# A fused attention and FFN kernel on eight cores: two FFN steps instead of one after an attention unit, and the attention epilogue due after 12 units instead of 14

## What is computed

```python
def reference(L0_attn_x, L0_attn_Wc_down, L0_attn_Wq_up, L0_attn_Wkv_up, L0_attn_Wc_proj,
              L0_ffn_w_gate, L0_ffn_w_up, L0_ffn_w_down):
    # x: (2, 8192, 1024) float32
    # attention: latent = x @ Wc_down (1024 -> 512); q = latent @ Wq_up (16 heads of 64);
    # one k and one v of 64 for all heads = latent @ Wkv_up; causal softmax(q k / 8) v;
    # then @ Wc_proj
    # ffn: h = silu(x @ wg.T) * (x @ wu.T), 3072 wide, then h @ wd.T; int weights times 1/127
    x = L0_attn_x
    xn = _layernorm(x, axis=-1)
    s = _L0_attn_ref(xn, ...)
    g = _silu(_L0_ffn_ref(xn, ...))
    x = x + s * g
    return x
```

## Time and profile before

| what | value |
|---|---|
| median of the runs (2 runs, 3182.01 to 3184.77) | 3183.39 us |
| the profiled execution's own time | 3173.12 us |
| its span on the slowest core (core 5) | 3171.3 us |
| spans of all cores | 3142.9 to 3171.3 us |
| granted TensorE clock, mean over the span, all cores | 0.818 to 0.830 of full speed |
| PE busy, ACT busy, DVE busy, POOL busy | 65%, 41%, 37%, 13% of the span |

### The profile page before, as it was taken

One profiled execution on the slowest core, in us unless ns is written; L12 is line 12 of the kernel. 1 busy time (PEld: TensorE's weight loads), 2 busy tenths in 40 slices (PEclk: granted clock), 3 DMA queues, 4 the chain that ended last, 5 costly groups with the idle time before them and its releaser, 6 DMA issues.

```text
span 3171.3 us, 32995 instructions; the slowest of 8 cores (3142.9 to 3171.3 us)
## 1 busy us (share of the span) xinstructions
PE 2066.2 (65%) x10464; PEld 990.6 (31%) x10464; DVE 1169.4 (37%) x1852; ACT 1311.0 (41%) x1457; POOL 416.6 (13%) x329
## 2 busy tenths in 40 slices
PE   1334536555575675785758758597585887578875
PEld 1112313222342342442225322252221542223521
DVE  4635434243543436435253251432422331511221
ACT  0111222222432433433634437355365437476465
POOL 0211122223243001101101101000111011011011
PEclk9556767687797896997879978699787998799998
DMA  5132274949687153351025300163001350012600
GB/s 97 29 55 54 35 105 51 141 100 136 78 87 136 50 130 110 85 145 35 29 49 135 99 23 21 43 143 97 15 15 48 74 155 21 23 28 56 152 28 14
DMA packets 547254, 232.12 MB, mean 73 GB/s; under 512 B 476432, under 2 KB 532752, under 8 KB 547088
## 3 DMA queue, kind: packets, MB, share of 16 engines
q1 hardware_dynamic: 429760, 186.88, 23.0%
q0 software_dynamic: 117328, 43.14, 12.8%
HBM read 241.62 MB, written 27.26 MB: 85 GB/s over the span
## 4 chain that ended last, share of the span: by engine, by line
PE 42%; DVE 20%; ACT 11%; DMA 11%; issue 10%; POOL 5%; DVEq 1%; SPq 0%; ACTq 0%; POOLq 0%
ACT p_sb L578 10%; PE ps_y L554 9%; PE ps_sc L567 9%; PE ps_u L725 6%; PE ps_u L796 5%; PE ps_u L732 5%; POOL p_sb L586 5%; DVE recbf L606 4%; DMA wu_t<-wu 2%; DMA xt<-xb 2%; PE ps_u L644 2%; DVE stat L306 2%; DVE h_sb L743 2%; DVE xnT L380 2%; DVE o_sb L814 1%
## 5 line engine op out<-in xcount | busy, mean ns | idle before, releaser
L578 ACT ACTIVATE p_sb<-ps_sc 128x1024 bf16<-128x1024 f32 x1088 | 1092.5, 1024 | 1287.1 <-PE ps_sc L567 1278.3
L554 PE MATMUL ps_y<-p_sb,vaug_sb 128*65 128x512 bf16 x2176 | 731.9, 421 | 255.3 <-POOL p_sb L586 153.4
L567 PE MATMUL ps_sc<-qs,kT_sb 65*128 65x512 bf16 x2176 | 730.3, 420 | 16.1 <-DVE qs L534 16.1
L586 POOL TENSOR_TENSOR p_sb<-p_sb,masks_sb 128x1024 bf16<-128x1024 bf16 x128 | 276.6, 2172 | 2232.9 <-ACT p_sb L578 2232.8
L554 PEld LDWEIGHTS ps_y<-p_sb,vaug_sb 128*65 128x65 bf16 x2176 | 209.7, 119 | 687.9 <-issue 609.3
L373 PE MATMUL ps_u<-ident_sb,xn_t 128*128 128x128 bf16 x512 | 65.5, 271 | 411.9 <-DVE xn_t L336 232.6
L567 PEld LDWEIGHTS ps_sc<-qs,kT_sb 65*128 65x128 bf16 x2176 | 220.4, 106 | 218.7 <-issue 74.6
L725 PE MATMUL ps_u<-xnT_own,wg_t 128*128 128x256 bf16 x1536 | 220.6, 291 | 88.8 <-DVE h_sb L743 62.1
L796 PE MATMUL ps_u<-wd_t,h_sb 128*128 128x512 bf16 x768 | 196.3, 403 | 70.9 <-DVE o_sb L814 25.0
L596 DVE CAST yf<-ps_y 64x1024 bf16<-64x1024 f32 x32 | 38.8, 1213 | 526.7 <-PE ps_y L554 526.7
L739 DVE SCALAR_TENSOR_TENSOR th<-t_sb,ps_u 128x256 bf16<-128x256 f32 x192 | 80.9, 421 | 405.0 <-ACT t_sb L736 404.5
(11 more groups left out here) (86 smaller groups left out, 1228.3 us busy)
## 6 DMA issues: line engine op xcount, KB each, us to landing
wg_t<-wgbf SPq DMA_DIRECT2D x144, 256.0 KB, 3.6
wu_t<-wubf SPq DMA_DIRECT2D x144, 256.0 KB, 4.1
wd_t<-wdbf SPq DMA_DIRECT2D x288, 128.0 KB, 2.4
xt<-xb SPq DMA_DIRECT2D x64, 512.0 KB, 4.6
wg_t<-wg POOLq DMA_DIRECT2D x48, 256.0 KB, 8.0
wu_t<-wu POOLq DMA_DIRECT2D x48, 256.0 KB, 8.6
wd_t<-wd POOLq DMA_DIRECT2D x96, 128.0 KB, 5.0
xo_t<-xo SPq DMA_DIRECT2D x16, 512.0 KB, 4.0
```

Of the source, the lines that this page charges most:

```text
L554: last = O("tensor", lambda e_, t=t, nh=nh, par=par: e_.matmul(ps_y[0:65, nh * 512:(nh + 1) * 512], vaug_sb[:, t, :], p_sb[:, par, nh * 51 ...
L567: sct = O("tensor", lambda e_, t=t, nh=nh, sb2=sb2: e_.matmul(ps_sc[:, sb2 * 1024 + nh * 512:sb2 * 1024 + (nh + 1) * 512], kT_sb[0:65, t * ...
L578: ex = O("scalar", lambda e_, sb2=sb2: e_.activation(p_sb[:, sb2, :], ps_sc[:, sb2 * 1024:(sb2 + 1) * 1024], AF.Exp), [sct, st["p_war"][sb ...
L586: mtoks[t] = O("gpsimd", lambda e_, pview=pview, mj=mj: e_.tensor_tensor(pview, pview, masks_sb[:, mj, :].unsqueeze(1).broadcast_to([128, ...
```

## The change

Two numbers. An active FFN generator advances by two yields per call, so two F steps or two D steps are written between two attention units where one was, and epilogues and projections are due after 12 calls of `pump()` instead of 14.

```diff
@@ -862,9 +862,9 @@
-        EPI_DELAY = 14
-
-        LAZY_STEPS = 1
+        EPI_DELAY = 12
+
+        LAZY_STEPS = 2
```

## The result

The changed kernel takes 3329.2 us (median of 11 runs, 3324.8 to 3370.4), the kernel before in the same session 3182.0 (median of 10). The ratio is 1.0493, with an interval of 1.0455 to 1.0532. By the medians it is slower by 147 us. In some executions, of kernels with one step per call too, the cores of one die show a lower granted clock (0.76 beside 0.82 in one of the kernel before, of 3254.9 us) and the time is longer; the ratios and, from the experiments on, the medians, ranges and numbers of runs leave these out, so that a ratio is not quite the quotient of the medians beside it. The profiled execution of after has its own time of 3341.5 us; its slowest core is core 1, with a span of 3339.8. The kernel before had core 5 as its slowest.

A forecast was written before the change was run, and what follows sets the result against it. FFN steps were taken as bound by chains of waits across engines, with no engine full. 3173.1 + 149.5 (plain units) + 16 (pass ends) + 3 (loads) = 3341.6; from the median 3351.9, stated as 3350 us, range 3305 to 3405.

The forecast's parts named there:

- What bounds the kernel: F steps: 3.0 us set by the chain gate, tanh, two DVE products, not PE's work; D steps likewise 4.29 us.
- Two steps per call: Pairs take 6.0 (F) or 8.6 us (D) and cover one attention unit; 130 units become plain at 1.15: 149.5 us.
- a sign: PE idle before L725 was to rise from 88.8 us by 86 us or more in the profile after.
- Another sign: In the last odd blocks, stretches of 42 plain units were to stand where 26 were.
- Ends of passes: At pass and block ends plain units cost more, as PE waits for POOL's masks: together 16 us.
- The first two generators: DMA-bound loads: D steps about +20, F pairs between transposes -6, block 4's 11.18 us stall gone -11; about +3 us.
- Epilogue: Due after 12 units, its product comes 2.3 us earlier with 9 us still to spare after the reciprocal: 0.
- Queues: Each F pair issues four weight loads in a row on SP, at the same pace of use and depth: 0.
- A: The second step does not wait: F pairs 4.35 us, D pairs about 6.0, total 3108 us; chance 0.03.
- B: Longer PE idle in F and D pairs brings the clock to 1.2 GHz: +128, 3480 us; chance 0.07.
- C: DMA bounds more of the first generators, at their upper bound of +50: 3400 us; chance 0.07.
- D: Freed plain units are covered by other work (LN, projection), so time stays at 3183 us; chance 0.03.

## Why the prediction was right

The forecast was 3350 us, and 3329.2 was measured, within the range of 3305 to 3405 and of the stated sign.

*What bounds the kernel.* Right, and shown. The step of 3.0 us is the chain through tanh and the two DVE products: with the gate's wait moved to L739 it fell to 2.61, with no other edit.

*Two steps per call.* Right in mechanism and size. Pairs are 5.99 and 8.58 us against 6.0 and 8.6; the idle in the middle is 1.08 and 1.54 against 1.1 and 1.5; a plain unit 1.15. The count of 130 is that of the ledger. The idle in front of L725 rose by 65 us on core 5 (88.8 to 153.5), less than the 86 or more that I named as a sign: the sign did not allow for the waits that go, those of 11.18 and 8.12 us among them. Against L743 alone it rose by 68.9. Another sign was put too sharply: the plain stretches did not go from 26 to 42 units but from 16 to 30 in block 13 and from 40 to 54 in block 15 (exponentials in a row with no other matmuls between them, core 5).

*Ends of passes.* Right within what can be seen: plain units together cost 196.0 against 197.8. The ledger does not part the ends from the rest.

*The first two generators.* This is the term that was mis-sized. Its parts on core 5: D steps of the first generator, predicted +20, came to about +24 (what stands above 4.29 each went from 37.8 to 41.2, and 21.0 of the former was the end of a pass, which a step of the next generator now covers). The stall, predicted -11, was -12.4, but the one that went was a wait of 8.12 us for the first gate tile, and not one for the products behind `xo_t`. The F steps, predicted -6, were -22. And one thing was not in the sum at all: the first D steps of blocks 6 and 7 had stood 5.0 and 4.8 us above 4.29, with waits of 3.67 and 4.01 us for tiles in them, and in pairs they don't. These four make 24 - 12 - 22 - 10 = -20, where the sum had +3, so 23 below it; all units with steps together came out 16 below the prediction on core 5, and 10 below it in the mean of the eight cores, so 7 us on core 5 went the other way, which I did not trace. I had counted only those F steps that newly meet a loaded tile near the transposes, at 4.2 us each. I had missed that with two steps per call the generator's F part is over earlier, so that the eight at 7.2 us each of the earlier trace rows stand no more at its end, and the pairs that remain in block 3 have a block's beginning before them in which to load.

*Epilogue.* Right: 0.9995 by itself.

*Queues.* Right for this kernel: no new wait for `wgbf` or `wubf` in after. With pairs at 5.0 us such waits came, in the run with the cut gate wait.

*The sum against the profiled execution.* The 168.4 us between the two profiled executions is the sum of 168.5 only by two misses that cancel: the loads cost less, and core 1 of after ran partly at a lower clock. The figures to hold it against are the medians, +147, and the mean of the cores' spans, +160.6. So the sum was 8 to 21 us too high, and the term of the loads (+3 in the sum) is where most of that lies.

*The rivals.* A (the second step doesn't wait) is refuted by the 1.08 idle. B (the clock falls because of the idle time in pairs) is refuted where it was placed: gate matmuls at 1.03 us behind idle times of 1.08 in pairs and in triples. C (DMA bounds more) has the wrong sign for this kernel; with three per call the D steps move that way. D (invisible) is refuted by the +147 and by the dose.

## What to carry to other kernels

Before you change how two streams are interleaved, find out which step's length is a chain of waits. Work that fits in the wait costs nothing there, and each piece taken out of it costs its full price elsewhere: here 1.1 to 1.3 us a unit in four kernels with 96 to 174 such units. The gain is in the other direction: shorten the chain (a wait for the last reader of just that half of a buffer gave 1.1%), and look at once at what is late next, which here was a load that waited for its buffer.

## What the runs showed of the hardware that I had not expected

Core 1 of after has stretches in which the granted clock is 0.81, which is neither of the two levels (2.4 GHz, at 1.00, and 1.2). They lie among F and D pairs like those that run at 1.00 elsewhere on the same core. Windows of core 1 (us, then PE, PEld, DVE, ACT and POOL busy (count), clock, DMA share, GB/s):

```profile
1446.00:1454.00 8.00, 5.97 (x24) 2.17 (x22) 2.42 (x4) 1.02 (x1) 0.00 (x0) 0.81 0.53 156
2204.00:2246.00 42.00, 33.14 (x247) 23.44 (x248) 10.99 (x27) 13.34 (x20) 0.00 (x0) 1.00 0.67 159
```

And the timeline of its down matmuls in a stretch that is at 0.81:

```profile
1831.55 3.31 PE L796 MATMUL ps_u<-wd_t,h_sb 128*128 128x512 bf16 x12 [0.49 <-DVE o_sb L814]
1836.40 3.31 PE L796 MATMUL ps_u<-wd_t,h_sb 128*128 128x512 bf16 x12 [1.54 <-DVE o_sb L814]
1841.25 3.31 PE L796 MATMUL ps_u<-wd_t,h_sb 128*128 128x512 bf16 x12 [0.49 <-DVE o_sb L814]
```

Twelve matmuls take 3.31 us where they took 2.75, and the D pair 9.70 us, not 8.58; F pairs there take 6.3. Added up from the clock's records in the trace, this level (0.8125 there) stands for 294, 293, 194 and 194 us on cores 0 to 3 of after, on cores 2 and 3 at other places of the span than on cores 0 and 1, and nowhere on the other die. The same holds for the profiled executions of four other kernels with pairs or triples (three per call, pairs with the cut gate wait, pairs from the second generator on, F pairs only), each time on die 0 alone, for 99 to 527 us a core; the five profiled executions with one step per call have none. Two with pairs have none either: the change without the epilogue's part, whose profiled execution took 3328.1, and pairs with both chains cut. It fits that the profiled execution of after is 12 us above the median. That pairs bring it on is not shown: there is one execution with a trace for each of the twelve kernels, and the 0.76 named with the result, with one step per call, is of an execution that left no trace to tell the level.

The Trainium skill, "TensorE: Matmul & The Clock Gate", section "Seeing it yourself", has a rule for this: a peak-current limiter takes a whole die to 13/16 of the clock once three of its cores run dense matmuls. The 0.8125 is 13/16, and the one die agrees; that cores 2 and 3 have it for 194 us and cores 0 and 1 for 294, and at other places, is not explained by the rule as it stands.

The second surprise is that two queues did not bring the tiles sooner: with 57.8 us of waits, POOL's queue beside SP's was no better than SP's alone with 41.1 (and tiles in pairs). The Trainium skill, "DMA: Bandwidth & Descriptors", section "Issuing engines are not separate DMA queues", says that starting transfers from several engines saves only the time to start them. The trace agrees in that this time was small, 0.36 us of SP in the row above; what made the tiles late there was the wait for a buffer.
